# Rotated values of the sharing heads from rounded parts, in a decoder layer in fp32

## Chip, cores and metric

One core of a Trainium2 chip runs the whole kernel. The metric is the time on the device in microseconds, the median of the runs. TensorE is the matmul engine, VectorE, ScalarE and GpSimd (POOL) compute elementwise, SyncE (SP) issues most DMAs. An engine works its own queue in order and meets the others at semaphores.

## What is computed

A decoder layer on x (8 x 128 x 512, fp32) with a context of the same shape: three blocks, each followed by a layer norm of its input plus the block's output. Cut to what matters:

```python
x = layernorm(x + polynomial_and_ffn(x))      # 128 wide polynomial, SwiGLU of 1248
h = rmsnorm(x) * ln_weight                    # 32 heads of 128
score = (h @ w_q.T) @ (ctx @ w_k.T).T + bias  # per batch and head
p = where(m, softmax(where(m, score, -inf)), 0)
x = layernorm(x + x + p @ (ctx @ w_v.T) @ w_out.T)
x = layernorm(x + ffn(x))                     # SwiGLU of 1376, weights in {-1, 0, 1}, scaled
```

In these inputs the attention mask leaves at most the last 32 of 128 keys of each batch.

## The kernel before

The 8 batches are two halves of 4 x 128 rows. The first block runs over tiles of 128 inner features, for one half and then the other; the attention runs over 64 head-halves n = 0 to 63 (called heads here); the last block runs again over tiles of inner features (11 a half), first half 0, then half 1.

**Parts.** A matmul in fp32r takes operands rounded to fewer bits. To keep fp32's accuracy an operand is split: ScalarE copies it to an fp32r tile (`_hi`), VectorE subtracts that from the whole (`_lo`), and `passes` (L551) issues hi x hi, hi x lo, lo x hi. Where an operand stays whole, TensorE gets an fp32 matmul, which the trace shows as two records.

**Two branches.** A flag worked out on the chip says whether keys ahead of the last 32 are in use. Where they aren't, as here, `attention(True)` runs on 128 keys (4 batches x 32) of each half. A second flag says whether the last block's weights have low bits; here they have none, and `last_block(False)` runs, in which a_lo and b_lo are not used, though the gate and `down` still wait for them. Only TensorE branches; the other engines have one program for both, so loads and copies that the short path doesn't use are made all the same.

**Order of heads.** Heads 0 to 15 belong to half 0, 16 to 31 to half 1, 32 to 47 to half 1 again (other weights), 48 to 63 to half 0. Heads 0 to 15 and 32 to 47 are `shared`: their keys and values are computed for both halves at once from rounded parts, and the other half's part is kept (`kept_k`, `kept_v`) for the head 16 later. Keys lead by 7 heads, queries by 6.

**One round of TensorE in a sharing head n**: `queries(n+6)` (L709), `turn(n-1)` (a transpose of the probabilities, L784), `weigh(n-2)` (rotated values by probabilities into `acc`, L847), `keys(n+7)` (L678, nothing where head n+7 doesn't share), `values(n)` (L797), `outer(n-1)` (the rotation: values by the head's output weight `wo`, L823), and, where n % 4 is 1 or 2, half of the next four heads' scores (`group_scores`, L752). In a head that doesn't share, `outer` reads `kept_v`, and the wait of `values` on its weight stays.

**One round of ScalarE** (L1215): copy_queries (t_ring, L1180), copy_turned (prob_t, L1187), split_k (wk_hi), copy_keys (kept_k, k_ring), split_v (wv_hi, in b_hi), copy_values (kept_v, v_sb, L1206), copy_outer (u_sb, L1213), exponentials (prob, L1194). `values(n)` waits for prob_t of head n-1, since both use one bank; `weigh(n-2)` waits for u_sb. **VectorE** (L1590): find_max, divide (row_sum, reciprocal, prob), add_mask, rest_k, rest_v.

**Loads.** SyncE issues, in each round n, wqi and wq of head n+8 (`load_q`, behind queries(n+6)), wk of n+10 (behind keys(n+7)), wo of n+2 (behind weigh(n-2)), wv of n+2 (behind values(n)), each 256 KB, and the bias of four heads once in four rounds, which the short path doesn't read.

**Last block.** Each step f has `gate`, `up` and `down` on TensorE; silu, a_hi, b_hi, tile_hi on ScalarE; a_lo, the product (L1370), b_lo, tile_lo on VectorE. `residual(4)` and `residual(5)` (L1402) empty the four accumulators of a finished part and stand between a product and b_lo; after residual(5) POOL adds four tiles of 128x512 (`add_scaled`, L526), then VectorE takes the moments and POOL normalises.

Of the kernel before, what the change touches and what calls it, by code (L numbers as in the profile page):

```python
# [71 lines left out]
WO_RING, WK_RING = 4, 3  # L72
# [47 lines left out]
def decoder_kernel(nc, xT, ctxT, ctxF, x_tok, mask, consts, ad, a1, b1, ax, wqn, wvh, bx, bias, biasF, w3, out):  # L120
    with ExitStack() as ctx:
# [9 lines left out]

        a_raw, a_hi, a_lo = two("a_raw", [P, 2 * C * P]), two("a_hi", [P, 2, C, P], F32R), two("a_lo", [P, 2, C, P], F32R)
# [48 lines left out]
        bias_sb = two("bias_sb", [P, GH * P])  # L181
# [3 lines left out]
        piece = [raw.bitcast(I32) for raw in piece_raw]  # L185
        mask_words = sb("mask_words", [P, BATCH, SEQ // 4], U32)
        mask_u8 = mask_words[:].bitcast(U8)
        mask_add = [sb(f"mask_add{j}", [P, BATCH, P], BF16) for j in range(GH)]
        few_add, key_scale = sb("few_add", [P, BATCH, FEW]), sb("key_scale", [P, 2])
# [38 lines left out]
        bias_dma = [sem("bias_dma0"), sem("bias_dma1")]  # L228
# [25 lines left out]
        few_dma, few_hi_ok, few_lo_ok, ctx_dma = sem("few_dma"), sem("few_hi_ok"), sem("few_lo_ok"), sem("ctx_dma")  # L254
        many_ok, keys_flag_ok = sem("many_ok"), sem("keys_flag_ok")
# [24 lines left out]
        def _(sp):  # L280
# [13 lines left out]
            def load_bias(g):  # L294

                if g >= 2:
                    sp.wait_ge(score_mm, (g - 1) * GH)
                sp.dma_start(bias_sb[g % 2][:], bias[head_of(g * GH) // GH]).then_inc(bias_dma[g % 2], 16)

            def load_q(n):  # L300

                if n >= 2:
                    sp.wait_ge(t_mm, n - 1)
                sp.dma_start(wqi[n % 2][:], ax[head_of(n)][:, 0:D]).then_inc(wqi_dma[n % 2], 16)
                sp.dma_start(wq[n % 2][:], wqn[head_of(n)]).then_inc(wq_dma[n % 2], 16)

            def load_k(n):

                if n == WK_RING - 1:
                    sp.wait_ge(hidden_ok, HALVES * F1)  # L310
                if n >= WK_RING:
                    sp.wait_ge(k_mm, n - WK_RING + 1)
                sp.dma_start(wk[n % WK_RING][:], ax[head_of(n)][:, D:]).then_inc(wk_dma[n % WK_RING], 16)

            def load_v(n):

                if n >= 2:
                    sp.wait_ge(v_mm, n - 1)
                sp.dma_start(wv[n % 2][:], wvh[head_of(n)]).then_inc(wv_dma[n % 2], 16)
# [59 lines left out]
            for n in range(2):  # L379
                load_v(n)  # L380
                load_bias(n)
# [3 lines left out]
            for n in range(-LEAD_K, HN):  # L385
# [16 lines left out]
                if n % GH == 1 and 2 <= n // GH + 2 < HALVES * GROUPS:  # L402
                    load_bias(n // GH + 2)
# [33 lines left out]
        def _(pool):  # L437
# [85 lines left out]
            pool.tensor_copy(low_flag[:], piece_all[:, 1:2]).then_inc(flag_ok, 1)  # L523
            normalise(2)
# [8 lines left out]
            for t in range(TT):  # L533
                add_scaled(5, t)
# [15 lines left out]
        def _(pe):  # L550
# [40 lines left out]
            def gate(a, par, half, done, low=True, last=False):  # L591
                pe.wait_ge(a_lo_ok, a + 2)
# [84 lines left out]
            def attention(few):  # L677
                def keys(n):  # L678
# [3 lines left out]
                    pe.wait_ge(wk_dma[raw], 16 * (n // WK_RING + 1))  # L682
# [26 lines left out]
                def queries(n):  # L709
# [5 lines left out]
                    pe.wait_ge(wqi_dma[par], 16 * (n // 2 + 1))  # L715
# [20 lines left out]
                def add_bias(n, g, j):  # L736
# [8 lines left out]
                    else:  # L745
                        pe.wait_ge(bias_dma[g % 2], 16 * (g // 2 + 1))
                        rows = bias_sb[g % 2][:].rearrange("p (h k) -> p h k", h=GH)
# [75 lines left out]
                def outer(n):  # L823
# [7 lines left out]
                    pe.wait_ge(kept_k_ok, shared_count(min(n + LEAD_K + 1, HN - 1)))  # L831
                    if few:
                        pe.wait_ge(wo_dma[slot], 16 * (n // WO_RING + 1))
                        if shared(n):
                            few_values = v_sb[par][:, half * P:(half + 1) * P]
                        else:
                            pe.wait_ge(kept_v_ok, shared_count(n - BLOCK))
                            few_values = kept_v[n % BLOCK]
                        mm = pe.matmul(bank[1][:], few_values, wo[slot][:], start=True, stop=True)  # L839
# [101 lines left out]
            pe.wait_ge(ctx_dma, HALVES * 16)  # L941
            pe.wait_ge(keys_flag_ok, 1)
            many_keys = pe.value_load(keys_flag[0:1, 0:1], min_val=0, max_val=1)
# [54 lines left out]
            pe.wait_ge(flag_ok, 1)  # L998
            has_low = pe.value_load(low_flag[0:1, 0:1], min_val=0, max_val=LOW_BITS)
            with pe.If(has_low < 1):  # L1000
                last_block(False)
            with pe.Else():
                last_block(True)
# [3 lines left out]
        def _(act):  # L1007
# [74 lines left out]
            def split_v(n):  # L1082
# [6 lines left out]
                act.activation(wv_hi[n % 2], wv[n % 2][:], ACT.Copy).then_inc(wv_hi_ok, 1)  # L1089

# [105 lines left out]
            def copy_values(n):  # L1196
# [9 lines left out]
                act.activation(v_sb[n % 2][:], bank[3][:], ACT.Copy).then_inc(v_ok, 1)  # L1206

# [7 lines left out]
            for n in range(-LEAD_K, HN):  # L1215
# [89 lines left out]
        def _(dve):  # L1305
# [49 lines left out]

            def few_bias_rests():
# [413 lines left out]
```

## Time and profile before

| | us |
|---|---|
| median of 3 runs | 741.21 (740.92 to 741.48) |
| profiled execution | 742.11 |
| its span in the trace | 740.3 |
| TensorE busy | 711.6 |
| VectorE busy | 522.3 |
| ScalarE busy | 409.2 |
| POOL busy | 95.1 |

The span goes from the first to the last instruction of the trace. Stages, in us of the span: first block to 222, keys and queries ahead of head 0 to 250, sharing heads to about 350, heads 16 to 31 to about 430, sharing heads to about 530, heads 48 to 63 to 600, last block to 729, then the end of the last layer norm. A row's time on TensorE contains the latency of the array, so records overlap; the distance between starts is what a matmul costs. "Granted clock" 1.00 is the full one.

### The profile page before, as it was taken

To read this page: it belongs to the slowest core of one execution; us is meant where nothing else is said; L and a number is where in the kernel's file an instruction comes from. 1 tells how busy PE (TensorE), PEld (TensorE's weight loads), DVE (VectorE), ACT (ScalarE), POOL (GpSimd) and SP (SyncE) were. 2 spreads that over 40 slices of the span, in tenths; PEclk is the share of its full clock that TensorE was granted. 3 is DMA by queue.
4 is the path that set the end of the run, shared out by engine and by line. 5 is a ranking of instruction groups with operands and counts; after the bars stand their busy time and mean duration, and the time that the engine had idled before them with its cause. 6 is when DMAs were issued, how large, how long until landed. Compare 5 with 4: busy or idle time off the path is not lost.

```text
span 740.3 us, 12271 instructions
## 1 busy us (share of the span) xinstructions
PE 711.6 (96%) x4082; PEld 555.6 (75%) x4082; DVE 522.3 (71%) x848; ACT 409.2 (55%) x747; POOL 95.1 (13%) x88
## 2 busy tenths in 40 slices
PE   9999999999999999999999999999989989998993
PEld 6788888888878888777667777877756548887882
DVE  6556587578765775776977786577699958569565
ACT  6342333333255666766776676667667654553542
POOL 2000000065001800000000000000040005006403
PEclk9999999999999999999999999999999999999998
DMA  8455532446565756667998786567796534442631
GB/s 296 164 203 202 179 143 71 139 151 217 188 214 175 259 180 200 211 229 230 289 320 267 249 257 193 185 224 248 231 324 233 166 105 128 147 151 88 210 114 58
DMA packets 70681, 145.10 MB, mean 196 GB/s; under 512 B 7920, under 2 KB 8192, under 8 KB 69984
## 3 DMA queue, kind: packets, MB, share of 16 engines
q1 hardware_dynamic: 69200, 137.26, 56.7%
q0 software_dynamic: 1200, 6.70, 2.3%
q8 instruction: 34, 0.56, 0.3%
q10 hardware_dynamic: 224, 0.39, 0.2%
q14 instruction: 23, 0.19, 0.1%
HBM read 142.23 MB, written 2.10 MB: 195 GB/s over the span
## 4 chain that ended last, share of the span: by engine, by line
PE 83%; DVE 7%; DMA 3%; issue 3%; ACT 2%; POOL 1%; SPq 0%; ACTq 0%; PEld 0%; DVEq 0%; POOLq 0%
PE bank L555 37%; PE acc L555 16%; PE acc L861 7%; PE bank L764 7%; PE bank L729 6%; PE bank L839 6%; PE bank L742 1%; DMA b_raw<-b 1%; DVE score L1564 1%; DVE neg_max L1570 1%; PE bank L791 1%; DMA a_raw<-a 1%; PE bank L588 1%; DVE row_sum L1578 1%; DMA wv<-wvh 1%
## 5 line engine op out<-in xcount | busy, mean ns | idle before, releaser
L1308 DVE TENSOR_TENSOR a_lo<-a_raw,a_hi 128x1024 fp32r<-128x1024 f32 (+3 forms) x47 | 56.9, 1210 | 84.4 <-ACT a_hi L1020 77.0
L555 PE MATMUL bank<-feat_hi,a_hi 128*128 128x512 f32 x260 | 102.5, 394 | 0.1
L555 PE MATMUL bank<-feat_lo,a_hi 128*128 128x512 f32 x260 | 101.8, 392 | 0.0
L555 PE MATMUL acc<-b_hi,tile_hi 128*128 128x512 f32 x224 | 88.0, 393 | 3.5 <-issue 1.9
L555 PE MATMUL acc<-b_hi,tile_lo 128*128 128x512 f32 x224 | 87.6, 391 | 0.0
L861 PE MATMUL acc<-u_sb,prob_t 32*128 32x512 f32 x512 | 73.2, 639 | 2.5 <-DMA wv<-wvh 1.3
L1037 ACT ACTIVATE tile_hi<-pair 128x512 fp32r<-128x512 f32 x54 | 33.9, 628 | 65.2 <-DVE pair L1370 36.3
L764 PEld LDWEIGHTS bank<-t_ring,xn 128*128 128x128 f32 x512 | 62.1, 192 | 8.5 <-issue 7.2
L457 POOL TENSOR_SCALAR scale<-moments 128x4 f32<-128x4 f32 (+1 forms) x9 | 2.6, 289 | 504.7 <-DVEq L1440 504.4
L555 PE MATMUL bank<-feat_hi,a_lo 128*128 128x512 f32 x172 | 67.0, 389 | 0.0
L1180 ACT ACTIVATE t_ring<-bank 128x512 f32<-128x512 f32 x64 | 38.2, 597 | 51.2 <-PE bank L729 51.0
L1578 DVE TENSOR_REDUCE row_sum<-prob 128x4 f32<-128x512 f32 x64 | 43.7, 683 | 27.6 <-ACT prob L1194 26.3
L764 PE MATMUL bank<-t_ring,xn 128*128 128x128 f32 x512 | 62.3, 275 | 0.0
L555 PEld LDWEIGHTS bank<-feat_hi,a_hi 128*128 128x128 f32 x260 | 49.3, 190 | 11.8 <-DVE a_lo L1308 1.5
L555 PEld LDWEIGHTS bank<-feat_lo,a_hi 128*128 128x128 f32 x260 | 49.3, 189 | 10.0
L555 PE MATMUL acc<-b_lo,tile_hi 128*128 128x512 f32 x136 | 52.9, 389 | 0.0
L555 PEld LDWEIGHTS acc<-b_hi,tile_hi 128*128 128x128 f32 x224 | 42.1, 188 | 13.9 <-issue 2.8
L1308 DVE TENSOR_TENSOR b_lo<-b_raw,b_hi 128x512 fp32r<-128x512 f32 x56 | 40.1, 715 | 14.9 <-ACT b_hi L1027 14.6
L1027 ACT ACTIVATE b_hi<-b_raw 128x512 fp32r<-128x512 f32 x56 | 34.8, 623 | 26.8 <-PE acc L555 21.3
L1046 ACT ACTIVATE gated<-bank 128x512 f32<-128x512 f32 x20 | 12.0, 598 | 67.8 <-PE bank L555 67.8
L555 PEld LDWEIGHTS acc<-b_hi,tile_lo 128*128 128x128 f32 x224 | 42.2, 188 | 8.7
L1020 ACT ACTIVATE a_hi<-a_raw 128x1024 fp32r<-128x1024 f32 x43 | 45.2, 1052 | 1.7 <-DMA a_raw<-a 1.6
(160 smaller groups left out, 1656.8 us busy)
## 6 DMA issues: line engine op xcount, KB each, us to landing
wqi<-ax SPq DMA_DIRECT2D x64, 256.0 KB, 3.3
wq<-wqn SPq DMA_DIRECT2D x64, 256.0 KB, 3.7
wv<-wvh SPq DMA_DIRECT2D x64, 256.0 KB, 4.1
wo<-bx SPq DMA_DIRECT2D x64, 256.0 KB, 3.9
a_raw<-w SPq DMA_DIRECT2D x22, 512.0 KB, 3.9
wk<-ax SPq DMA_DIRECT2D x43, 256.0 KB, 3.8
a_raw<-a SPq DMA_DIRECT2D x21, 512.0 KB, 5.3
b_raw<-b SPq DMA_DIRECT2D x34, 256.0 KB, 2.7
```

What stands on the lines that cost most here:

```text
L555: mm = pe.matmul(out_ap, w, x, start=start and k == 0, stop=stop and k == len(products) - 1, skip_group_check=True)
L729: mm = pe.matmul(bank[0][:, c * P:(c + 1) * P], wq[par][:, c * P:(c + 1) * P], few_keys, start=True, stop=True)
L764: mm = pe.matmul(bank[2][:, b * P:(b + 1) * P].rearrange("p (k h) -> p h k", h=GH), xn[half][:, c, b * SEQ:(b + 1) * SEQ], t_ring[g % 2][: ...
L839: mm = pe.matmul(bank[1][:], few_values, wo[slot][:], start=True, stop=True)
L861: mm = pe.matmul(acc[b][:], prob_t[par][rows, 0:P], u_sb[par][rows, :], start=begins, stop=ends, skip_group_check=True)
L1020: act.activation(a_hi[par][:].rearrange("p w c k -> p (w c k)"), a_raw[par][:], ACT.Copy).then_inc(a_hi_ok, 1)
L1027: act.activation(b_hi[par][:], b_raw[par][:], ACT.Copy).then_inc(b_hi_ok, 1)
L1037: act.activation(tile_hi[par][:], src, ACT.Copy).then_inc(tile_hi_ok, 1)
L1046: act.activation(gated[:], bank[0][:], ACT.Silu).then_inc(silu_ok, 1)
L1180: act.activation(t_ring[n // GH % 2][:, n % GH].rearrange("p c b k -> p (c b k)"), bank[0][:], ACT.Copy).then_inc(t_ok, 1)
L1308: return dve.tensor_tensor(out_ap, whole, high, ALU.subtract)
L1578: dve.tensor_reduce(row_sum[:], prob[n % 2][:], AX_X, ALU.add).then_inc(sum_ok, 1)
```

## The change

For the 32 sharing heads `outer` takes rounded parts of both operands. ScalarE gains `split_o` (wo_hi) at the head of its round and v_hi behind v_sb, VectorE gains `rest_values` (v_lo, 128x128) and, for heads 0 and 1, `rest_o`; from head 2 on POOL makes wo_lo, behind VectorE's key rest of the same round, or behind the next head's normalised prob where there is none. The new tiles lie where others are dead (a_raw0, the mask, few_add), wo's ring goes from 4 to 3 and its load from head n+2 to n+1, the bias keeps one buffer; the load of the last block's first a_raw goes from round 32 to round 50. wq is loaded ahead of wqi. In the short path TensorE no longer waits for loads that it doesn't use, and SyncE waits for a slot's last load in its place. The short path stands first in its branch, and the last block is called inside each. Where weights have no low bits, `gate` and `down` wait for the rounded part alone. residual(4) goes ahead of the product of its step, residual(5) and the moments behind tile_lo, the second moments one step later, and POOL's third and fourth sum of part 5 wait for the second half's step 1.

```diff
-WO_RING, WK_RING = 4, 3
+WO_RING, WK_RING = 3, 3
+POOL_O = 2
...
             def load_q(n):
...
+                sp.dma_start(wq[n % 2][:], wqn[head_of(n)]).then_inc(wq_dma[n % 2], 16)
+                if n >= 2:
+                    sp.wait_ge(wqi_dma[n % 2], 16 * (n // 2))
                 sp.dma_start(wqi[n % 2][:], ax[head_of(n)][:, 0:D]).then_inc(wqi_dma[n % 2], 16)
-                sp.dma_start(wq[n % 2][:], wqn[head_of(n)]).then_inc(wq_dma[n % 2], 16)
...
-                if WO_RING <= n + 2 < HN:
-                    load_o(n + 2)
+                if WO_RING <= n + 1 < HN:
+                    load_o(n + 1)
...
-                if n == 2 * BLOCK:
-                    sp.wait_ge(few_lo_ok, 1)
+                if n == 3 * BLOCK + 2:
+                    sp.wait_ge(u_mm, 3 * BLOCK)
                     load_a(A30, A30 % 2, w3[0][:, 0:2 * D])
...
+            for n in range(POOL_O, HN):
+                if shared(n):
+                    pool.wait_ge(wo_hi_ok, shared_count(n))
+                    if n % GH < GH - 1 and n + LEAD_K + 1 < HN and shared(n + LEAD_K + 1):
+                        pool.wait_ge(wk_lo_ok, shared_count(n + LEAD_K + 1))
+                    else:
+                        pool.wait_ge(prob_ok, n + 1)
+                    pool.tensor_tensor(wo_lo[n % 2][:], wo[n % WO_RING][:], wo_hi[n % 2][:].bitcast(F32),
+                                       ALU.subtract).then_inc(wo_rest_ok, 1)
             normalise(2)
...
             for t in range(TT):
+                if t == TT // 2:
+                    pool.wait_ge(hidden_ok, HALVES * F1 + F3 + 2)
                 add_scaled(5, t)
...
-                pe.wait_ge(b_lo_ok, m + 1)
+                pe.wait_ge(b_lo_ok if low else b_hi_ok, m + 1)
...
-                pe.wait_ge(a_lo_ok, a + 2)
+                pe.wait_ge(a_lo_ok if low else a_hi_ok, a + 2)
...
-                    pe.wait_ge(wv_dma[par], 16 * (n // 2 + 1))
+                    if not few or shared(n) or n >= HN - 2:
+                        pe.wait_ge(wv_dma[par], 16 * (n // 2 + 1))
...
+                    if shared(n):
+                        pe.wait_ge(v_lo_ok, shared_count(n))
+                        if n < POOL_O:
+                            pe.wait_ge(wo_lo_ok, n + 1)
+                        else:
+                            pe.wait_ge(wo_rest_ok, shared_count(n) - POOL_O)
...
-                            few_values = v_sb[par][:, half * P:(half + 1) * P]
+                            mm = passes(bank[1][:], v_hi[par][:], v_lo[par][:], wo_hi[par][:], wo_lo[par][:], True, True)
...
-            with pe.If(many_keys > 0):
-                attention(False)
-            with pe.Else():
-                attention(True)
+            with pe.If(many_keys < 1):
+                attention(True)
+                streamed()
+            with pe.Else():
+                attention(False)
+                streamed()
...
+            def split_o(n):
+
+                act.wait_ge(wo_dma[n % WO_RING], 16 * (n // WO_RING + 1))
+                if n >= 2:
+                    act.wait_ge(u_mm, n - 1)
+                act.activation(wo_hi[n % 2][:], wo[n % WO_RING][:], ACT.Copy).then_inc(wo_hi_ok, 1)
...
+                if shared(n):
+                    own = half_of(n)
+                    act.wait_ge(v_ok, n + 1)
+                    act.activation(v_hi[n % 2][:], v_sb[n % 2][:, own * P:(own + 1) * P], ACT.Copy).then_inc(v_hi_ok, 1)
...
+                if n >= 0 and not late:
+                    split_o(n)
...
+            def rest_values(n):
+
+                own = half_of(n)
+                dve.wait_ge(v_hi_ok, shared_count(n))
+                low(v_lo[n % 2][:], v_sb[n % 2][:, own * P:(own + 1) * P], v_hi[n % 2][:].bitcast(F32)).then_inc(v_lo_ok, 1)
...
                     find_max(m)
+                if n >= 1 and shared(n - 1):
+                    rest_values(n - 1)
                 if n >= 0:
                     divide(n)
...
-            step3(1, 1, 0, after=lambda: residual(4))
-            step3(2, 2, 0, after=lambda: variances(3))
+            step3(1, 1, 0, before=lambda: residual(4))
+            step3(2, 2, 0, behind=lambda: variances(3))
...
-            step3(0, 0, 1, after=lambda: residual(5))
-            step3(1, 1, 1, after=lambda: variances(4))
-            step3(2, 2, 1)
+            step3(0, 0, 1, behind=lambda: residual(5))
+            step3(1, 1, 1)
+            step3(2, 2, 1, behind=lambda: variances(4))
```

`before` stands ahead of the product of a step and behind a_lo, `after` between product and b_lo, `behind` at the step's end.

## Rows read from the trace of the kernel before

**Rows 1.** Page, part 1: busy us (share of the span) xinstructions

```profile
PE 711.6 (96%) x4082; PEld 555.6 (75%) x4082; DVE 522.3 (71%) x848; ACT 409.2 (55%) x747; POOL 95.1 (13%) x88
```

**Rows 2.** Chain, a sharing head: start us, us, what

```profile
269.16 3.06 PE bank L555 x24
272.22 0.86 PE bank L839 x2
```

**Rows 3.** Chain, last block

```profile
642.72 1.81 PE acc L555 x8
644.53 3.63 PE bank L555 x16
...
673.64 2.59 PE acc L555 x8
676.24 4.75 PE bank L555 x16
```

**Rows 4.** Chain, a sharing head without keys

```profile
331.78 0.89 PE bank L729 x8
...
332.79 1.07 PE acc L861 x8
333.86 0.15 issue
```

**Rows 5.** Timeline: start us, us, engine, line, op, [idle before <-releaser]

```profile
329.27 0.43 SPq L325 DMA_DIRECT2D wo<-bx  x1
...
330.96 0.28 ACT L1203 ACTIVATE kept_v<-bank 128x128 f32<-128x128 f32 x1 [0.80 <-PE bank L555]
331.13 0.59 ACT L1206 ACTIVATE v_sb<-bank 128x512 f32<-128x512 f32 x1
...
331.82 0.60 ACT L1213 ACTIVATE u_sb<-bank 128x512 f32<-128x512 f32 x1
...
332.31 0.62 ACT L1194 ACTIVATE prob<-score 128x512 f32<-128x512 f32 x1
...
332.83 0.59 ACT L1180 ACTIVATE t_ring<-bank 128x512 f32<-128x512 f32 x1
...
333.31 0.60 ACT L1187 ACTIVATE prob_t<-bank 128x512 f32<-128x512 f32 x1
...
333.90 0.69 DVE L1582 TENSOR_TENSOR prob<-prob,row_inv 128x512 f32<-128x512 f32 x1
```

**Rows 6.** DMA issues, 261 to 300 us; last number: us to landing

```profile
wo<-bx SPq DMA_DIRECT2D x6, 256.0 KB, 3.4
```

**Rows 7.** Timeline, hand-over of halves in the last block

```profile
668.01 2.48 DVE L1421 TENSOR_TENSOR normed<-acc,ad_sb 128x512 f32<-128x512 f32 x4
...
668.77 5.92 POOL L530 TENSOR_TENSOR resid<-normed,resid 128x512 f32<-128x512 f32 x4 [38.68 <-DVE normed L1421]
...
670.40 1.47 DVE L1308 TENSOR_TENSOR b_lo<-b_raw,b_hi 128x512 fp32r<-128x512 f32 x1
...
671.80 1.75 DVE L1308 TENSOR_TENSOR tile_lo<-pair,tile_hi 128x512 fp32r<-128x512 f32 x1
...
673.64 0.47 PE L555 MATMUL acc<-b_hi,tile_hi 128*128 128x512 f32 x1 [1.89 <-issue]
```

**Rows 8.** DMA issues, 345 to 375 us, heads that share nothing

```profile
wo<-bx SPq DMA_DIRECT2D x7, 256.0 KB, 5.2
```

**Rows 9.** Timeline of PE, round 21

```profile
371.95 1.14 PE L861 MATMUL acc<-u_sb,prob_t 32*128 32x512 f32 x8 [1.33 <-DMA wv<-wvh]
```

**Rows 10.** Timeline, keys ahead of head 0

```profile
233.50 1.13 PE L729 MATMUL bank<-k_ring,wq 128*128 128x128 f32 x8 [0.74 <-DMA wq<-wqn]
```

**Rows 11.** Timeline, first keys behind the branch

```profile
222.26 0.36 PE L555 MATMUL bank<-a_hi,wk_hi 128*128 128x256 f32 x1 [1.56 <-issue]
```

**Rows 12.** Timeline, entry of the last block

```profile
609.48 0.50 PE L555 MATMUL bank<-last_hi,a_hi 128*128 128x512 f32 x1 [1.18 <-DVE a_lo L1308]
```

**Rows 13.** Windows: us, PE, PEld, DVE, ACT, POOL, clock, DMA, GB/s

```profile
676.00:682.00 6.00, 6.00 (x22) 4.70 (x22) 5.66 (x13) 2.79 (x4) 2.44 (x3) 0.80 0.15 38
```

More of the change, by code:

```diff
@@ L129, in sem @@
             return ctx.enter_context(nc.semaphore(name))
+        with ExitStack() as sharing:
+            wo_hi = [sharing.enter_context(nc.sbuf_tensor(f"wo_hi{i}", [P, D], F32R)) for i in range(2)]
         a_raw, a_hi, a_lo = two("a_raw", [P, 2 * C * P]), two("a_hi", [P, 2, C, P], F32R), two("a_lo", [P, 2, C, P], F32R)
@@ L180, in decoder_kernel @@
         prob_t = two("prob_t", [P, N])
-        bias_sb = two("bias_sb", [P, GH * P])
+        bias_sb, wo_lo = sb("bias_sb", [P, GH * P]), two("wo_lo", [P, D], F32R)
         piece_raw = [prob_t[0][:], prob_t[1][:], prob[0][:].rearrange("p b k -> p (b k)"), prob[1][:].rearrange("p b k -> p (b k)"),
@@ L185, in decoder_kernel @@
         piece = [raw.bitcast(I32) for raw in piece_raw]
+        with ExitStack() as sharing:
+            v_hi = [sharing.enter_context(nc.sbuf_tensor(f"v_hi{i}", [P, P], F32R)) for i in range(2)]
         mask_words = sb("mask_words", [P, BATCH, SEQ // 4], U32)
@@ L188, in decoder_kernel @@
         mask_add = [sb(f"mask_add{j}", [P, BATCH, P], BF16) for j in range(GH)]
+        with ExitStack() as sharing:
+            v_lo = [sharing.enter_context(nc.sbuf_tensor(f"v_lo{i}", [P, P], F32R)) for i in range(2)]
         few_add, key_scale = sb("few_add", [P, BATCH, FEW]), sb("key_scale", [P, 2])
@@ L294, in load_bias @@
             def load_bias(g):
[L296 to L298 removed]
+                if g >= 1:
+                    sp.wait_ge(score_mm, g * GH)
+                sp.dma_start(bias_sb[:], bias[head_of(g * GH) // GH]).then_inc(bias_dma, 16)
             def load_q(n):
@@ L380, in _ @@
                 load_v(n)
-                load_bias(n)
+            load_bias(0)
             load_o(0)
@@ L681, in keys @@
                     keys_bank = bank[keys_in(n)]
-                    pe.wait_ge(wk_dma[raw], 16 * (n // WK_RING + 1))
+                    if not few or shared(n) or n >= HN - WK_RING:
+                        pe.wait_ge(wk_dma[raw], 16 * (n // WK_RING + 1))
                     if shared(n):
@@ L714, in queries @@
                     pe.wait_ge(wq_dma[par], 16 * (n // 2 + 1))
-                    pe.wait_ge(wqi_dma[par], 16 * (n // 2 + 1))
+                    if not few or n >= HN - 2:
+                        pe.wait_ge(wqi_dma[par], 16 * (n // 2 + 1))
                     if n == 0:
@@ L834, in outer @@
                         if shared(n):
-                            few_values = v_sb[par][:, half * P:(half + 1) * P]
+                            mm = passes(bank[1][:], v_hi[par][:], v_lo[par][:], wo_hi[par][:], wo_lo[par][:], True, True)
                         else:
                             pe.wait_ge(kept_v_ok, shared_count(n - BLOCK))
-                            few_values = kept_v[n % BLOCK]
-                        mm = pe.matmul(bank[1][:], few_values, wo[slot][:], start=True, stop=True)
+                            mm = pe.matmul(bank[1][:], kept_v[n % BLOCK], wo[slot][:], start=True, stop=True)
                     else:
@@ L1354, in rest_v, with rest_o @@
                 low(wv_lo[n % 2], wv[n % 2][:], wv_hi[n % 2].bitcast(F32)).then_inc(wv_lo_ok, 1)
+            def rest_values(n):
+                own = half_of(n)
+                dve.wait_ge(v_hi_ok, shared_count(n))
+                low(v_lo[n % 2][:], v_sb[n % 2][:, own * P:(own + 1) * P], v_hi[n % 2][:].bitcast(F32)).then_inc(v_lo_ok, 1)
+            def rest_o(n):
+                dve.wait_ge(wo_hi_ok, n + 1)
+                low(wo_lo[n % 2][:], wo[n % WO_RING][:], wo_hi[n % 2][:].bitcast(F32)).then_inc(wo_lo_ok, 1)
             def few_bias_rests():
@@ L1373, in product, with feed @@
                     dve.tensor_tensor(hidden[mpar], bank[1][:], gated[:], ALU.mult).then_inc(hidden_ok, 1)
-            def feed(a, apar, m, mpar, done, last_block=False, f=0, split_next=True, before=None, after=None):
+            def feed(a, apar, m, mpar, done, last_block=False, f=0, split_next=True, before=None, after=None,
+                     behind=None):
                 if split_next:
@@ L1386, in feed @@
                 tile_rest(m, mpar, hidden[mpar])
+                if behind is not None:
+                    behind()
             def chunk(p, c, bank_):
@@ L1629, in _, with step3 @@
             s0 = HALVES * F1
-            def step3(f, sf, h, split_next=True, after=None):
+            def step3(f, sf, h, split_next=True, before=None, behind=None):
                 feed(f + (A30 + h * F3), (A30 + h * F3 + sf) % 2, f + (T30 + h * F3), (T30 + h * F3 + sf) % 2,
-                     f + (s0 + h * F3), last_block=True, f=f, split_next=split_next, after=after)
+                     f + (s0 + h * F3), last_block=True, f=f, split_next=split_next, before=before, behind=behind)
             split_a(A30 + 1, (A30 + 1) % 2)
```

33 lines of the change are left out of this document (20 added, 13 removed).

## The prediction

> **What bounds the kernel now.** I read the table of engines first. TensorE is busy for 711.6 of 740.3 us [rows 1], so a microsecond is won only where TensorE gets less work or waits less, and any other engine costs something only where TensorE waits for it. Next comes the chain that ended last, stage by stage. In the sharing stages (heads 0 to 15 and 32 to 47) a head with keys has 24 matmuls of keys and values in 3.06 us and the rotation (output weight by values, two records of a plain fp32 matmul) in 0.86 us [rows 2]. In the last block everything goes by rounded parts: eight matmuls of 512 columns take 1.81 us and sixteen 3.63 [rows 3]. In the second half of a sharing stage no keys are left (they lead by seven heads); there the chain has queries 0.89, weighing 1.07 and a gap of 0.15 in front of the values [rows 4]. The timeline says whose gap that is: ScalarE's copy prob_t runs from 333.31 for 0.60 us, which is when TensorE may start the values [rows 5]. So there ScalarE's queue is already the bound, by a hair, in heads that are not followed by group scores.
>
> **The rotation itself.** Three matmuls of rounded parts replace two records: 3 x 1.81/8 = 0.68 us [rows 3] for 0.86 [rows 2], a gain of 0.18 us in each of 32 sharing heads, 5.8 us if everything else stays covered.
>
> **What feeds it.** ScalarE gets two more instructions a head: wo_hi, 128x512, at the head of its round, and v_hi, 128x128, between v_sb and u_sb, where it must first wait for v_sb to end. VectorE gets the rest of v_hi (a quarter of an instruction of 0.69 us, ahead of a product of probabilities for which it has to wait for ScalarE anyway: nothing, and 0.69 us a head if it had no such wait), POOL the rest of wo_hi (VectorE for heads 0 and 1); behind POOL's rests only normalise(2) is queued, whose moments come after the last of them. Count from kept_v at 330.96 [rows 5]. Today v_sb follows at +0.17, u_sb +0.86, prob +1.35, t_ring +1.87, prob_t +2.35, and the next kept_v comes at +4.75. Afterwards v_sb ends at +0.76, v_hi starts near +0.80, u_sb, 0.17 behind it, at +0.97, prob at +1.46, wo_hi at +1.98, t_ring at +2.50, prob_t at +2.98: 0.63 later than today. Three kinds of head follow.
> - With group scores behind the rotation (1.78 us of TensorE's time), or at a stage's end: the additions are covered. 20 rotations, each -0.18: -3.6 us.
> - With keys but no group scores: values come 1.53 us later (half of 3.06), so prob_t is covered, but u_sb now ends at +1.57, and a released weighing starts some 0.15 later, at +1.72, where TensorE would be there at about +1.57. Six heads at -0.18 + 0.15: -0.2 us.
> - Without keys and without group scores (9, 12, 13 and 41, 44, 45): the 0.63 goes straight into the period. wo must have landed too. Its load is now issued one head later: 329.27 is 1.69 before kept_v [rows 5], and it takes 3.4 us at the median [rows 6], so it lands at +1.71, just ahead of the +1.98 where ScalarE wants it; with the scatter I take 0.75 for 0.63. POOL's rest waits for the next head's normalised prob: that starts 1.59 behind the exponential and takes 0.69 [rows 5], so POOL starts at about +3.8 and, at 5.92/4 = 1.48 us [rows 7], ends at +5.3, where the rotation wants it at about +5.2: another 0.1. Six heads at +0.85: +5.1 us.
>
> Together +1.3 us. The ends are -5.8 (all covered) and +7.0 (each of the twelve heads without group scores loses another half microsecond to a late wo). I take the middle since the recurrence reproduces today's 4.75.
>
> **The order of loads.** wo's ring shrinks from four to three and the bias from two buffers to one; the latter is not read on the path that runs. New waits on the SyncE queue (a slot's earlier load of wqi, wk, wv must have landed) have the head's wk, wo and wv queued behind them. They look two or three heads back, at least 6.2 us, and loads land in 3.4 to 5.2 [rows 6, 8], so they cost nothing while landing stays there. Those waits leave TensorE, which no longer stands on loads that it doesn't use: 1.33 us on wv at 371.95 [rows 9]; what is late next is wo, issued just ahead of wv, now one head less early. I take -1.0 there, and +0.3 for the 512 KB load of the last block's first weights, moved from head 32 into the crowded stretch at head 50 (0 to 1.8 us, by which a landing in the crowded stretch exceeds one in the sharing stage). wq goes ahead of wqi: 0.74 us of TensorE's waiting on it [rows 10], one of two such rows, the other with 0.78; an issue is 0.43 us [rows 5], so -0.8 for both (0 to -1.5).
>
> **The branches.** TensorE sits 1.56 us idle ahead of the first keys, at 222.26, with every operand there [rows 11]: it reads the flag and jumps over the long path, which now lies behind the one that runs. Reading a flag alone is hidden at the second branch, behind a weighing like that of [rows 4], 1.07 us, since the next matmul follows it without a gap. The transposes ahead of the first branch cover less than half of that, so I leave the reading some 0.7 and take the rest for the jump: -0.9 (0 to -1.6).
>
> **The last block, entry.** The gate no longer waits for a_lo, which isn't used there: 1.18 us at 609.48 [rows 12]. But residual(4), 4 x 0.62 by the row of residual(5) [rows 7], now stands ahead of the product, so the next "up" waits for it instead: VectorE ends a_lo at 609.4, the residual at about 612.0, the product at 612.8. TensorE would be back at "down" some 0.4 us earlier than now: -0.4 (0 to -1.2).
>
> **The hand-over of halves.** This is the largest term. VectorE takes residual(5) (2.48 us), which sets POOL's four sums off at 668.77, and then b_lo and tile_lo, at 1.47 and 1.75 us beside POOL [rows 7], where 0.68 is usual for both. TensorE, done with "up", sits idle for 1.89 us until 673.64 [rows 7], and then runs eight matmuls in 2.59 and sixteen in 4.75 us instead of 1.81 and 3.63: another 1.9 [rows 3]. The granted clock from 676 to 682 is 0.80 of the upper level (2.4 GHz) [rows 13], so part of it ran at the lower one (1.2 GHz), right behind that idle stretch. In the new order residual(5) comes behind tile_lo, which then ends near 669.5, before POOL starts; the accumulators are free at 672.0, TensorE asks for the last at about 673. POOL's other two sums wait for the next product and then meet b_lo and tile_lo of step 1, which have 3.63 us of gate and "up" as cover. -3.8 (the clock's share alone may stay: -1.9 to -3.8). What queues behind POOL's new wait is normalise(4) and the stores, done long before the end.
>
> **A rule against it.** In the trace POOL's sums leave `normed<-acc,ad_sb` alone, 2.48 us for four though POOL starts in their midst, but stretch b_lo and tile_lo by 0.8 and 1.1 us [rows 7]. The Trainium skill, SBUF — State Buffer, "Who interferes with whom", says why: an instruction of VectorE with two SBUF inputs and a POOL instruction that reads SBUF exclude each other for a whole instruction. By that rule POOL's 30 new rests are late by up to one VectorE subtraction. That is the third rival; its price stands there.
>
> **Sum.** +1.3 - 1.0 + 0.3 - 0.8 - 0.9 - 0.4 - 3.8 = -5.3 us. The profiled execution took 742.11 us (its span 740.3 and 1.8 around it), which becomes 736.8; it is 0.9 above the median of the runs, 741.21, which becomes 735.9.
>
> **Rivals.** (1) Everything is covered: ScalarE catches up and the rotations give their 5.8 us: 735.9 - 7.1 = 728.8. For it: ScalarE idles 0.80 us before kept_v even in these heads. Against: that idling lies behind prob_t, not ahead. Chance 0.20. (2) wo becomes the bound, and the kernel slower. The place is ScalarE's wo_hi at the head of its round. If landing rises from 3.4 to 4.4 us (it is 5.2 in the crowded stretch [rows 8]), t_ring and prob_t start up to 1.2 later: 6 heads with keys x 0.6, 4 without x 0.7, and some 2 us in the unshared heads, +8.5: 744.4. It decides from about 4.2 us on. Against: the sharing stages are the emptier ones. Chance 0.09. (3) POOL and VectorE block each other: the rest of wo is done 0.69 later, at +6.0, where the rotation wants it at +5.2: 0.8 x 6 heads = +4.8, 740.7. Chance 0.10. (4) The hand-over doesn't clear: the collision moves to the next step, tile_lo is late there and the clock falls there: 735.9 + 3.8 = 739.7. For it: POOL's sums are as long as before. Against: the cover of 3.63 us. Chance 0.14.
>
> **Numbers.** My forecast has 0.47. A measurement of this kernel can tell about 0.2% (1.5 us) from no change. Faster: 0.47 + 0.20 and half of rival 4 and a little of rival 3, 0.76; the same: 0.15; slower: rival 2, 0.09. The range, 728.5 to 741.0, takes in rivals 1, 3 and 4 and leaves out rival 2 and the outer ends.
>
> **What would show it.** Three records of about 0.23 us each for a rotation; periods of about 5.4 for 4.75 us in heads 12 and 13, with TensorE's values released by prob_t; a gap of 0.15 before weighing in heads with keys; no wait on wv; no gap over 0.5 us around 671 and no lower clock behind it; POOL's rests at 1.3 to 1.5 us. Wrong would be: wo_hi waiting on its load, rotations released by POOL's wo_lo, or heads without keys that still take 4.75.

## The result, and the profile after

The changed kernel takes 745.02 us (median; single runs from 743.0 to 749.2) against 741.21: a ratio of 1.0055, with a 95% interval of 1.0031 to 1.0079. It is slower by 4 us where 5 fewer were forecast. The profiled execution took 745.52 us, its span is 743.7.

The table of engines of the changed kernel, which answers [rows 1]:

```profile
PE 708.6 (95%) x4114; PEld 563.3 (76%) x4114; DVE 536.8 (72%) x882; ACT 432.5 (58%) x811; POOL 135.9 (18%) x118
```

TensorE has 3.0 us less to do and takes 3.4 us longer: it stands idle 6.4 us more than before. To find where, take the start of the first weighing matmul of each of the 64 heads in both traces and subtract. After minus before this difference is -1.3 us at head 0, near 0 from head 2 to head 10, +3.6 at head 11, +2.8 behind head 19, +3.1 at head 39, +7.8 at head 44 and +7.9 at head 63; at the end of the span it is +3.4. So the sharing stages lose, most of it in their ends without keys, and the last block gives 4.5 us back. Heads are counted here by their weighing. The stretch that ends with the weighing of head n holds the values of head n + 1, so the prediction's heads 12, 13, 41, 44 and 45 are heads 11, 12, 40, 43 and 44 here.

The largest single step is head 11. Timeline of the changed kernel, SyncE's issues, ScalarE and then TensorE (idle before and releaser in brackets):

```profile
324.65 0.43 SPq L341 DMA_DIRECT2D wo<-bx  x1
...
327.88 0.62 ACT L1240 ACTIVATE prob<-score 128x512 f32<-128x512 f32 x1
329.79 0.63 ACT L1135 ACTIVATE wo_hi<-wo 128x512 fp32r<-128x512 f32 x1 [1.29 <-DMA wo<-bx]
330.33 0.58 ACT L1226 ACTIVATE t_ring<-bank 128x512 f32<-128x512 f32 x1
330.81 0.59 ACT L1233 ACTIVATE prob_t<-bank 128x512 f32<-128x512 f32 x1
```

```profile
328.13 1.14 PE L897 MATMUL acc<-u_sb,prob_t 32*128 32x512 f32 x8
331.49 0.36 PE L583 MATMUL bank<-a_hi,b_hi 128*128 128x256 f32 x1 [2.22 <-issue]
...
332.34 0.41 PE L583 MATMUL bank<-a_hi,b_lo 128*128 128x256 f32 x1
332.56 0.41 PE L583 MATMUL bank<-a_hi,b_hi 128*128 128x256 f32 x1
```

The output weight is asked for at 324.65 and ScalarE can round it only at 329.79. The copies t_ring and prob_t are queued behind that rounding; in the kernel before they stood directly behind the exponential [rows 5]. TensorE, released by prob_t, stands still for 2.22 us. Then its matmuls of 256 columns start 0.21 us apart instead of 0.12. The windows say why (the value behind POOL's is the granted clock, 1.00 being the full one):

```profile
331.40:333.00 1.60, 1.51 (x9) 1.54 (x10) 0.57 (x1) 1.00 (x2) 0.37 (x1) 0.66 0.95 346
333.00:335.00 2.00, 2.00 (x8) 1.80 (x8) 1.41 (x3) 0.89 (x3) 0.00 (x0) 0.50 0.24 84
```

In the second window the clock is at its lower level, 1.2 GHz. Head 11 takes 8.19 us where it took 4.75. The waits that the profile puts down to this rounding, from 430 to 530 us:

```profile
ACT wo_hi L1135 <- DMA wo<-bx: 6.0, 7, 2.2
```

(us in total, times, longest), and 4.9 us in 7 waits from 250 to 350. Where the weight had landed in time, as at head 43, the period is 5.41 us for 4.75.

The last block is the other half of the story. Its steps stand 5 to 7 us later in this trace: the eight matmuls that start at 673.64, behind the stop, in the kernel before stand at 679.03 in the chain here. The chain and two windows of the changed kernel, to be held against [rows 3] and [rows 13]:

```profile
675.41 3.63 PE bank L583 x16
679.03 1.81 PE acc L583 x8
680.85 3.63 PE bank L583 x16
```

```profile
676.00:682.00 6.00, 6.00 (x28) 4.99 (x27) 5.86 (x8) 2.35 (x5) 2.66 (x3) 1.00 0.38 132
664.00:682.00 18.00, 18.00 (x85) 14.97 (x84) 14.28 (x20) 9.26 (x15) 2.66 (x3) 1.00 0.37 132
```

The hand-over of halves has no gap and no lower clock any more. VectorE's part, against [rows 7]:

```profile
675.29 0.68 DVE L1360 TENSOR_TENSOR b_lo<-b_raw,b_hi 128x512 fp32r<-128x512 f32 x1
...
676.14 0.69 DVE L1360 TENSOR_TENSOR tile_lo<-pair,tile_hi 128x512 fp32r<-128x512 f32 x1 [0.17 <-ACT tile_hi L1076]
...
676.75 2.48 DVE L1487 TENSOR_TENSOR normed<-acc,ad_sb 128x512 f32<-128x512 f32 x4
...
677.52 2.55 POOL L556 TENSOR_TENSOR resid<-normed,resid 128x512 f32<-128x512 f32 x2 [37.72 <-DVE normed L1487]
```

Both subtractions are done before POOL starts, as the new order wants it.

### The profile page after: what moved, and what is told of

The parts are those of the page before. It is cut to its first block, busy times and chain, and to the rows that moved or that the text cites. A ratio compares the mean times of both kernels' runs of the same rounds, so it can differ in the third digit from the quotient of the medians.

```text
span 743.7 us, 12618 instructions
## 1 busy us (share of the span) xinstructions
PE 708.6 (95%) x4114; PEld 563.3 (76%) x4114; DVE 536.8 (72%) x882; ACT 432.5 (58%) x811; POOL 135.9 (18%) x118
## 4 chain that ended last, share of the span: by engine, by line
PE 85%; DVE 6%; issue 4%; ACT 3%; POOL 1%; DMA 1%; SPq 0%; ACTq 0%; DVEq 0%; POOLq 0%
PE bank L583 41%; PE acc L583 18%; PE acc L897 7%; PE bank L794 6%; PE bank L759 6%; PE bank L875 3%; DVE row_sum L1644 1%; PE bank L616 1%; PE bank L772 1%; DVE score L1630 1%; DVE neg_max L1636 1%; PE bank L821 1%; DVE score L1638 1%; DMA stage<-xT 1%; POOL resid L556 1%
## 5 line engine op out<-in xcount | busy, mean ns | idle before, releaser
L548 POOL TENSOR_TENSOR wo_lo<-wo,wo_hi 128x512 fp32r<-128x512 f32 x30 | 38.9, 1297 | 236.0 <-DVE wk_lo L1360 128.1
L1360 DVE TENSOR_TENSOR b_lo<-wv,b_hi 128x512 fp32r<-128x512 f32 x32 | 26.2, 818 | 30.2 <-ACT b_hi L1128 30.2
```

Of the source, the lines that this page charges most:

```text
L548: pool.tensor_tensor(wo_lo[n % 2][:], wo[n % WO_RING][:], wo_hi[n % 2][:].bitcast(F32), ALU.subtract).then_inc(wo_rest_ok, 1)
L1360: return dve.tensor_tensor(out_ap, whole, high, ALU.subtract)
```

## The experiments

Theory A: the loss is ScalarE standing at the late output weight, with prob_t queued behind it. Theory B: it is the work of the rotation from parts itself (roundings, rests, POOL beside VectorE). Each run is compared with the kernel before on the same chip, whose medians there were 741.2 to 741.6 us.

**The weights one head earlier** (changed kernel). The fourth buffer is taken from wqi, which the path that runs doesn't read: it keeps one buffer, and each of its loads waits for the one before. So the path for many keys isn't kept, and the traffic is the same. Cut to the ring and the load:

```diff
-WO_RING, WK_RING = 3, 3
+WO_RING, WK_RING = 4, 3
...
-                if WO_RING <= n + 1 < HN:
-                    load_o(n + 1)
+                if WO_RING <= n + 2 < HN:
+                    load_o(n + 2)
```

> The changed kernel with its output weights loaded one head earlier, as in the kernel before: four buffers, load of head n+2 in round n (the fourth buffer is taken from the second one of the other loads of the keys' matrix, which the path that runs never reads; so that the path for many keys isn't kept, the traffic stays the same). Theory A, the landing of the output weight ahead of ScalarE's rounding is the lost time: the rounding no longer waits, the rises of heads 11, 31, 40, 42 and 44 fall from 3.4, 1.0, 1.0, 1.5 and 1.8 us to at most 0.7 each, no half clock near 331 us, and the total is 738 to 740 us. Rival B, the rotation from parts costs this by its own work on ScalarE, VectorE and POOL: 744 to 746 us, the rounding's waits gone and the rises still there.

738.89 us (737.3 to 740.1), ratio 0.9966 (0.9953 to 0.9979). The rounding waits for no load any more, head 11 takes 5.51 us, and no half clock follows. A holds for the larger part. Five rises are left in heads without keys (0.76, 0.53, 0.53, 0.66 and 0.52 us at heads 11, 12, 40, 43, 44). They have another shape; timeline of this run:

```profile
508.64 0.62 ACT L1135 ACTIVATE wo_hi<-wo 128x512 fp32r<-128x512 f32 x1
509.16 0.59 ACT L1226 ACTIVATE t_ring<-bank 128x512 f32<-128x512 f32 x1
...
509.64 0.60 ACT L1233 ACTIVATE prob_t<-bank 128x512 f32<-128x512 f32 x1
...
510.33 0.36 PE L583 MATMUL bank<-a_hi,b_hi 128*128 128x256 f32 x1 [0.83 <-issue]
```

Nothing is late here. ScalarE has no idle time ahead of these rows, and TensorE waits 0.83 us for its prob_t.

**The rounding later in ScalarE's round, the load left late:**

```diff
-                if n >= 0 and not late:
-                    split_o(n)
                 if 0 <= n + LEAD_T < HN:
                     copy_queries(n + LEAD_T)
...
                 if n >= 0:
                     copy_values(n)
+                if n >= 0 and not late:
+                    split_o(n)
```

> The changed kernel with the rounding of the output weight moved, in ScalarE's round, from ahead of the copy of the turned queries to behind the copy of the values, its load left late. Theory A (a late weight only hurts because prob_t and the copies are queued behind it): waits of the rounding vanish, as it stands 2 us later, total 738 to 741 us. Rival B (the rotation's own work): 744 to 746. Rival C (the value copies are pressed harder: u_sb comes 0.7 us later behind the rounding and the rotation's POOL rest starts later): rises in heads 9, 12, 13, 41 and 45 of 0.5 to 1 us each, total 742 to 748.

743.88 us (743.6 to 744.6). A alone would have given 738 to 741. The rounding no longer waits, but a new wait takes its place, which is rival C, in other heads than I had named: u_sb is now behind the rounding, and TensorE waits for it at heads 3, 6, 10, 11, 34, 35 and others, which grow by some 0.5 us each. Another stop, of 1.53 us, stands ahead of head 0, at 254.38: VectorE's rest of wo waits 0.88 us for the late rounding, and the rest of the next value weight, for which TensorE waits, is queued behind it. So this run moves the loss rather than removing it. Timeline of this run:

```profile
488.55 0.61 ACT L1135 ACTIVATE wo_hi<-wo 128x512 fp32r<-128x512 f32 x1
...
489.06 0.58 ACT L1263 ACTIVATE u_sb<-bank 128x512 f32<-128x512 f32 x1
...
489.79 1.14 PE L897 MATMUL acc<-u_sb,prob_t 32*128 32x512 f32 x8 [0.59 <-ACT u_sb L1263]
```

**All of the change but the rotation:** the matmul reads v_sb and wo again, and wo_hi, wo_lo, v_hi and v_lo are gone.

> The changed kernel with the rotation as in the kernel before (one fp32 matmul of v_sb and wo; no wo_hi, wo_lo, v_hi, v_lo), and all the rest kept: branches, waits, order of the loads, three buffers of output weights loaded late, the last block. From the trace of the changed kernel: start -1.3, the wait on wv -1.4, the last block -4.5, against 741.2: 734 us. If the late load of the output weight or the single bias buffer cost time by themselves, 736 to 738; if the time of the sharing stages isn't from the rotation at all, 744 to 745.

734.96 us (734.4 to 735.8), ratio 0.9915 (0.9898 to 0.9931). The rest of the change is worth 6.3 us; the rotation from parts, as it stands, costs 10.

**The edits of the last block alone, on the kernel before:**

> The kernel before with the edits of the last block alone (VectorE's two drains and two variances moved, POOL's wait ahead of the third sum, the narrower waits of gate and down). If these edits alone give what the trace of the changed kernel shows behind the attention (its end comes 4.5 us earlier against the attention's end): 736.7 us, no half clock between 675 and 679 us. If part of that was the branch or the moved load: 738 to 739. If the gain is only slack bought by the later attention: 741.

736.30 us (735.8 to 736.8), 5.0 us gained; no half clock between 664 and 682 us. The gain is that of these edits and not slack from the later attention. Its trace is 5.3 us shorter, and 4.4 us of that come behind head 63: 0.6 at the block's entry and 3.8 at the hand-over. Another 0.96 comes at head 19, where nothing was edited: the stop of 1.33 us on wv [rows 9] isn't in this execution.

**The old rotation, with the weights early again** (the two edits above together):

> The run with the old rotation and all the rest of the change, with the output weights loaded a head earlier again (four buffers, the fourth taken from the other loads of the keys' matrix, which the path that runs never reads; the path for many keys isn't kept). In the trace with the late load one rise is left that can be its own, 0.78 us at head 11. Theory A (without a rounding on ScalarE nobody but the rotation waits for the weight): 734.0 to 734.4 against 735.0, the 0.78 gone. Rival B (the late load costs time by itself in many heads): below 733. Rival C (the 0.78 has another cause): 735.0 and the rise still there.

734.28 us (734.1 to 734.8). The late load costs at most 0.7 us where only the rotation waits for it, and 6.1 (745.0 to 738.9) where ScalarE rounds it. The total is A's, the place isn't: in the traces 0.8 us of the difference lies ahead of 236 us, before any head, where runs with the same order of loads start between 235.4 and 236.8, and 0.60 of head 11's 0.78 us stay. Their cause is another load, on which ScalarE stands; timeline of this run:

```profile
329.22 0.63 ACT L1122 ACTIVATE b_hi<-wv 128x512 fp32r<-128x512 f32 x1 [1.76 <-DMA wv<-wvh]
```

**Only the rounding put back:** the old rotation, the late load, and split_o at its place; nobody reads wo_hi. Against the run with the old rotation:

```diff
+                if n >= 0 and not late:
+                    split_o(n)
                 if 0 <= n + LEAD_T < HN:
```

> The run with the old rotation, all the rest of the change and the late load (735.0 us), with one operation put back in each of the 32 sharing heads: ScalarE's rounding of the output weight, at its place in the queue; nobody reads what it writes. Theory A (the loss is ScalarE standing at the late weight ahead of the turned queries' and probabilities' copies, not the arithmetic of the rotation): it alone brings back most of the 10 us, 740 to 743, with TensorE's stops ahead of the values of heads without keys, and a wide spread. Rival B (it takes the parts' other work, v_hi, the rests and POOL): 735.5 to 737.

746.73 us (744.8 to 747.8), ratio 1.0068 (1.0045 to 1.0091): 11.8 us more than without it, above what I gave A. This one ScalarE instruction a head, with its late operand, is enough for the whole loss. Waits from 250 to 350 us, and its longest stop:

```profile
ACT wo_hi L1129 <- DMA wo<-bx: 9.2, 11, 2.3
```

```profile
515.93 0.63 ACT L1129 ACTIVATE wo_hi<-wo 128x512 fp32r<-128x512 f32 x1 [2.16 <-DMA wo<-bx]
...
517.63 0.35 PE L583 MATMUL bank<-a_hi,b_hi 128*128 128x256 f32 x1 [2.94 <-issue]
```

**Rounded parts in 18, in 8 and in 7 heads.** The next three use the parts only where a predicate says so, all with early weights. The one of 18 takes its fourth weight buffer as in the first experiment (and like it doesn't keep the path for many keys); those of 8 and 7 heads have wo_lo in one buffer and keep every path.

```diff
+def parted(n):
+    return n % GH < 2 and (4 <= n < 9 or 32 <= n < 41)
```

> As the changed kernel with its output weights loaded one head earlier, but the rotation comes from parts only in the 18 sharing heads that have keys of their own to compute in the same round (0 to 8, 32 to 40); the 14 others (9 to 15, 41 to 47) keep the fp32 matmul. Theory A (ScalarE is the bound where there are no keys: 5.45 us of it in a head of 4.64): the five rises of 0.5 to 0.8 us behind heads 10 and 42 go, 3.0 us of 738.9, total 735 to 736; rises left at heads 2 and 7 (0.4 and 0.7). Rival B (the excess of the medians comes from everywhere in the sharing heads): 737.5 to 739.

737.35 us (736.4 to 738.7), not the 735 to 736 of A. The five rises in heads without keys are gone as A had it, but head 2 now takes 8.81 us for 5.99:

```profile
270.61 3.45 POOL L556 TENSOR_TENSOR wo_lo<-wo,wo_hi 128x512 fp32r<-128x512 f32 x2 [8.06 <-issue]
```

```profile
272.63 0.47 PE L591 MATMUL bank<-wo_hi,v_hi 128*128 128x512 f32 x1 [1.99 <-POOL wo_lo L556]
```

POOL's first rest comes late, TensorE stands 1.99 us, and from 272.6 to 276.6 the granted clock is 0.63 in the mean. In the changed kernel the same stop is 1.31 us long, without a lower clock.

> As the run with rounded parts in the 18 heads with keys, but the rests of the output weights of heads 2 and 3 are made by VectorE too, POOL begins with head 4. Theory A (TensorE stood 2.0 us for POOL's first rest, behind which the clock was at half for about 3 us): the stop near 272 us and the half clock go, 737.3 - 2.5 = 734.8, between 734.3 and 735.5. Rival B (VectorE is now too full in heads 2 and 3: 1.4 us more): 736 to 737.

The same with `POOL_O = 4` in place of 2, so that VectorE makes the first four rests: 735.07 us (734.8 to 735.3). The stop and the half clock are gone: 2.3 us, as A says.

> All of the change, but the rotation comes from rounded parts only in the eight heads whose rotation lies beside a quarter of the group's scores and the keys' products (4, 5, 8, 32, 33, 36, 37, 40), where the trace of the changed kernel shows 0.16 us gained in each; the others keep the fp32 matmul. The output weights are loaded a head earlier, in four buffers; the fourth is paid by one buffer of wo_lo in place of two. Theory A (parts gain 0.16 where TensorE is the bound and lose where ScalarE is): 734.2 - 8 x 0.16 = 732.9, between 732.4 and 733.6. Rival B (rounding and rests cost time in heads with keys too, through ScalarE's queue or through POOL beside VectorE): 735 to 737.

733.68 us (733.6 to 734.0), ratio 0.9894 (0.9877 to 0.9912), 7.6 us less than before on the same chip; it beats both kernels, and its runs lie closest together. Over the old rotation with early weights (734.28) that is 0.6 us, about the scatter of that run's own executions. It misses A's 732.4 to 733.6 by a hair: seven heads are 0.16 us shorter, the eighth (40) isn't, and head 7 is 0.53 us longer, since the rounding for head 8 stands in the round of the features' copies.

> As the run with rounded parts in eight heads, without head 8: there the rounding stands on ScalarE in the round of the features' copies, and the trace shows 0.53 us lost ahead of head 7's weighing against 0.16 gained. Theory A: 733.7 - 0.4 = 733.3, between 732.9 and 733.6. Rival: that rise had another cause and stays, 733.8.

733.88 us (733.1 to 734.9): no difference that can be told from the eight. In the trace the 0.53 is gone (head 7 takes its 7.25 us again), but a late wv brings 0.44 at head 11. At this size the scatter of the loads decides, so this one is inconclusive.

**POOL without its waits on VectorE**, with early weights:

```diff
-                    if n % GH < GH - 1 and n + LEAD_K + 1 < HN and shared(n + LEAD_K + 1):
-                        pool.wait_ge(wk_lo_ok, shared_count(n + LEAD_K + 1))
-                    else:
-                        pool.wait_ge(prob_ok, n + 1)
```

> The changed kernel with its output weights loaded a head earlier, and POOL subtracts for wo_lo as soon as the rounding is done, no longer behind VectorE's rest of the key weights or behind its probabilities. Theory A (the wait costs head 2 and nothing else): POOL's first rest starts near 266.5 us in place of 269.8, head 2 is 0.4 us shorter, 738 to 739 against 738.9. Rival B (POOL and VectorE block each other): operations of VectorE with two operands in SBUF grow from 0.69 to 1.1 to 1.7 us where the rest runs beside them, the divisions come late, 740 to 743.

739.27 us (739.1 to 741.5) against 738.89 with the waits. The total is 0.3 above A's range, and its reason is wrong: head 2 takes 7.23 us, 0.9 more than with the waits. POOL's first rest starts not near 266.5 but at 270.88:

```profile
262.54 0.19 POOL L539 CAST low_flag<-piece_all 128x1 int32<-128x1 f32 x1
270.88 2.96 POOL L544 TENSOR_TENSOR wo_lo<-wo,wo_hi 128x512 fp32r<-128x512 f32 x2 [8.15 <-issue]
```

So neither VectorE nor the rounding (done at 266.3) holds it. B's contention is real, VectorE's busy time rises from 534.0 to 550.9 us, yet the median rises by 0.4 us only (the profiled executions differ by 1.7): VectorE isn't the bound.

**The changed kernel once more:**

> The changed kernel once more, beside these three. Its time again between 743 and 749 us. Theory A: the rounding of the output weight waits in ScalarE's queue for its DMA again, in sum 8 to 14 us in the sharing heads, and the spread comes from how long that wait is at a few heads; the half clock appears only where TensorE stood still for about 2 us. If the half clock near 331 us is there again without such a stop, it has another cause; if it is missing, the time is 742 to 743.

746.78 us (744.5 to 749.0). The longest stop of TensorE, 2.69 us ahead of 333.39, is this time not followed by the lower clock. For that case I had expected 742 to 743 us; the time is as long all the same, since weights are late at other heads too (head 14 is 1.7 us longer). The longest stop:

```profile
331.69 0.63 ACT L1135 ACTIVATE wo_hi<-wo 128x512 fp32r<-128x512 f32 x1 [1.75 <-DMA wo<-bx]
...
333.39 0.36 PE L583 MATMUL bank<-a_hi,b_hi 128*128 128x256 f32 x1 [2.69 <-issue]
```

**Where each run has its time.** Worked out from the starts of the first weighing matmuls, us against the kernel before:

| stretch between weighings | changed | again | early | rounding alone | old rotation | 8 heads |
|---|---|---|---|---|---|---|
| start to head 0 | -1.3 | -0.6 | -1.0 | -1.4 | -1.4 | -1.9 |
| 0 to 2 | +1.2 | +0.8 | +0.2 | 0.0 | 0.0 | 0.0 |
| 2 to 10 | +0.2 | +1.4 | 0.0 | +0.8 | 0.0 | +0.1 |
| 10 to 18 | +4.0 | +4.7 | +1.3 | +4.0 | +0.9 | 0.0 |
| 18 to 30 | -1.5 | -1.5 | -1.5 | -1.5 | -1.5 | -1.5 |
| 30 to 39 | +0.5 | +0.2 | -0.5 | +0.5 | 0.0 | -0.6 |
| 39 to 63 | +4.8 | +4.1 | +1.5 | +6.3 | +0.1 | 0.0 |
| sum | +7.9 | +9.1 | 0.0 | +8.7 | -1.8 | -3.9 |

## Why the prediction was wrong

The other six terms came to -6.3 us (735.0 less 741.3) for -6.6. The first, the rotation at +1.3 us (outer ends -5.8 and +7.0), measured +10.1 (745.0 less 735.0), above even its outer end, and most of that is rival 2.

- *The step that failed.* "wo must have landed too ... it takes 3.4 us at the median [rows 6], so it lands ... just ahead". The margin was worked out right: from the issue 1.69 before kept_v to the +1.98 where ScalarE wants the weight are 3.67 us. But [rows 6] was read from 261 to 300 us, and the heads that it was used for lie between 310 and 355, and from 485 to 530. There the trace of the same kernel before has a median of 4.1 us:

```profile
wo<-bx SPq DMA_DIRECT2D x8, 256.0 KB, 4.1
```

  and 3.9 in the second stretch. "Against: the sharing stages are the emptier ones" holds for their beginning alone. The late load by itself is worth 6.1 us (745.0 to 738.9).
- *The right row would have been half the answer.* At 4.1 us of landing the wait would have been 0.4 us. The changed kernel shows medians of 4.6 in both stretches, and 5.0 and 4.4 in its second trace, while its first heads keep 3.3. The two weights issued behind the weighings of heads 9 and 10 land in 5.1 and 5.3 us; in the kernel before it was 3.8 and 3.6, and 4.5 and 4.0 with the last block's edits alone. So the change lengthened landings, which the prediction took over from the kernel before. The old rotation with the changed loads shows it too (6.3 and 5.8): it isn't the rotation. One candidate is the bias load, 256 KB, which the prediction priced at nothing since nobody reads it. With one buffer it is issued behind the weighings of heads 9 and 13, and no longer of 7 and 11 (in the kernel before the first of them stands at 312.82):

```profile
326.76 0.43 SPq L310 DMA_DIRECT2D bias_sb<-bias  x1
```

  No run puts it back, nor the order of wq and wqi, so what lengthened the landings is not shown.
- *Rival 2.* It named the place on ScalarE and the threshold (4.2 us). Its chance of 0.09 came from the wrong row, and the range left it out on that ground. That its time fits (744.4 for 745.0) is in part luck: it put 3.6 us into heads with keys and 2 into unshared heads. The only head with keys where a late weight shows is 31 (1.0 us), and heads 18 to 30 lose nothing. The rest of what the late weight costs is in the heads without keys, and about 1.4 us of it is the clock.
- *What stood behind the term.* With the weights in time the rotation still costs 4.6 us in the medians (738.9 less 734.3) and 2.8 in the profiled executions, for +1.3. The gain of a covered rotation is 0.16 us and not 0.18, and it appears in 14 heads of the run with early weights, not in 20. Heads without keys lost 0.5 to 0.8 us in five cases for 0.85 in six: head 43's 5.41 us is the predicted recurrence to the hundredth (4.75 + 0.63), released by prob_t as foreseen. And four rises weren't in the sum at all: 0.8 to 0.9 us ahead of head 0, where TensorE waits for k_ring (0.43) and prob_t (0.37 to 0.46) behind the first roundings; 0.4 to 1.4 us at head 2 for POOL's first rest; 0.7 at head 7, where the copies of the features stand behind the rounding; and 0.3 at heads 17 and 49 each, the stages' ends that were taken as covered.
- *The clock.* That a stop of 2 us can bring the lower level I had used in the last block, as a gain, and not in the attention, as a price. At head 11 of the changed kernel it cost about 1.4 us: the head is 3.44 us longer, of which the stop is 2.22 for 0.15 [rows 4]; in the second trace a stop of 2.69 without it made the head 2.52 longer.
- *Loads and waits.* The wait on wv: -1.4 for -1.0, of which 0.96 also went in the run with the last block's edits alone, so what the edit itself gave is open between 0.4 and 1.4. The load moved to head 50: nothing for +0.3. A wv that lands late brings 0.4 to 0.8 us at head 11 in three runs with the changed loads and the old rotation there. The start (wq and branch) for -1.7: -0.9 to -2.2 in the four runs whose first heads have the old rotation and no rounding. The stop of 1.56 us [rows 11] is gone altogether, in the changed kernel the first keys start at 220.13 with no gap, and so are both waits on wq; but stops of 0.43 and 1.09 us ahead of later key products, at 231.96 and 235.60, have come.
- *The last block.* 4.4 us in the trace and 5.0 in the medians, alone, for 4.2: the entry 0.6 for 0.4, the hand-over 3.8 for 3.8. Predicted step by step, and right.
- *Rival 3.* POOL's rests last 1.3 us as forecast. By the Trainium skill, SBUF — State Buffer, "Who interferes with whom", VectorE with two SBUF inputs and a POOL instruction that reads SBUF exclude each other for a whole instruction. The run with the later rounding agrees: v_lo, 0.28 us alone, takes 1.36 beside a POOL rest of 1.32.

```profile
489.24 1.32 POOL L548 TENSOR_TENSOR wo_lo<-wo,wo_hi 128x512 fp32r<-128x512 f32 x1 [6.36 <-ACT wo_hi L1135]
489.34 1.36 DVE L1360 TENSOR_TENSOR v_lo<-v_sb,v_hi 128x128 fp32r<-128x128 f32 x1
```

  It costs little here: in the changed kernel TensorE waits for POOL's rest at head 2 alone, and in the run with the later rounding twice for v_lo, 0.36 us each.

What stays open: what lengthened the landings of the output weights, why the median of the run with early weights lies 1.3 us above its profiled execution (737.57), and what splits stops of TensorE into those with and those without the lower clock behind them.

## What to carry to other kernels

Before an operand's first reader is moved from the engine that uses it last to one that reads it early, compare the landing time of its load with the new margin, in the very stretch where it will be read: here 3.67 us of margin met 4.1 in the kernel before and 4.6 in the changed one. A margin within the scatter of landings is none, and a change that moves loads can move the landings too. Behind an in-order engine a late operand delays everything in the queue, also what never needed it: the same late load cost at most 0.7 us in front of TensorE and 6.1 in front of ScalarE. A cheaper form of an operation need not be used everywhere: used only where TensorE is the bound (8 of 32 heads) it kept its 0.16 us in seven heads, and lost 0.53 at one.

## What the hardware showed unexpectedly

- TensorE's clock falls after some stops and not after others of the same length. Stops of 1.99, 2.22 and 2.94 us in the attention were followed by 1.2 GHz, as the 1.89 of the last block before; one of 2.06 in the changed kernel's first trace (at 523.59), and 1.94 and 2.69 in its second, were not. What a stop costs is therefore a range: its own length, or that and 0.8 to 1.6 us more (the rise of the head less the stop, at the three stops of the attention with a lower clock).
- POOL's next large instruction comes late behind its all-reduce. In six traces it starts after 7.3 to 8.3 us of idle time behind the small copy that follows the all-reduce, with or without waits on VectorE; what POOL does in it the traces don't show. A rest that TensorE needs soon shouldn't be POOL's first.
